# Attention by query halves, and all eight PSUM banks in one pool, in a pre-norm transformer layer

## What is computed

```python
x = x + attn(layernorm(x))     # x: (2, 1024, 1024) fp32
x = x + ffn(layernorm(x))

def attn(x):                   # 32 heads, hd = 32, scale = 32 ** -0.5
    q, k, v = split(x @ qkvw + qkvb)
    probs = softmax(q @ k.T * scale)        # per head, 1024 x 1024
    return (probs @ v) @ ow + ob

def ffn(x):
    return (silu(x @ W_gate.T) * (x @ W_up.T)) @ W_down.T
```

## Time and profile before

| what | us |
|---|---|
| median of 3 runs (2999.91 to 3004.09) | 3000.97 |
| the profiled execution, its own time | 3001.82 |
| span of its profile | 3000.0 |
| TensorE busy in the span | 2954.2 (98%) |
| VectorE busy | 2180.4 (73%) |
| ScalarE busy | 1660.0 (55%) |
| GpSimd busy | 1393.7 (46%) |

### The profile page before, as it was taken

One profiled execution on the slowest core, in us unless ns is written; L12 is line 12 of the kernel. 1 busy time (PEld: TensorE's weight loads), 2 busy tenths in 40 slices (PEclk: granted clock), 3 DMA queues, 4 the chain that ended last, 5 costly groups with the idle time before them and its releaser, 6 DMA issues.

```text
span 3000.0 us, 39212 instructions
## 1 busy us (share of the span) xinstructions
PE 2954.2 (98%) x13728; PEld 2335.6 (78%) x13728; DVE 2180.4 (73%) x3175; ACT 1660.0 (55%) x3039; POOL 1393.7 (46%) x998
## 2 busy tenths in 40 slices
PE   7999999999999999999999999999999999999999
PEld 7777777777777777777677878888888888888887
DVE  6788888888788888888885488866665666555653
ACT  2588877778788888888874143333333323332221
POOL 1346555554555555556552244444354444535730
PEclk9999999999999999999999999999999999999999
DMA  5545445454454554645845735522532223857874
GB/s 205 173 135 163 142 139 184 131 170 128 128 174 131 156 169 140 192 130 150 253 134 178 240 109 193 189 102 100 233 135 100 100 104 118 262 177 252 268 244 132
DMA packets 328376, 492.10 MB, mean 164 GB/s; under 512 B 34746, under 2 KB 178234, under 8 KB 320116
## 3 DMA queue, kind: packets, MB, share of 16 engines
q1 hardware_dynamic: 328180, 489.60, 51.4%
HBM read 318.58 MB, written 169.87 MB: 163 GB/s over the span
## 4 chain that ended last, share of the span: by engine, by line
PE 89%; DVE 6%; DMA 1%; ACT 1%; issue 1%; POOL 1%; SPq 0%; DVEq 0%; ACTq 0%
PE ps L901 20%; PE ps L902 20%; PE ps L903 20%; PE ps L985 7%; PE ps L997 7%; PE ps L1002 7%; PE ps L969 7%; DVE mx L1342 1%; DVE pl L1364 1%; PE ps L935 1%; DVE wl L1316 1%; ACT ph L1124 0%; ACT pu L1123 0%; SPq L1634 0%; DVE bl L1427 0%
## 5 line engine op out<-in xcount | busy, mean ns | idle before, releaser
L1551 POOL TENSOR_TENSOR pl<-pu,ph 128x512 fp32r<-128x512 f32 x504 | 679.6, 1350 | 677.8 <-ACT ph L1124 677.5
L1342 DVE TENSOR_REDUCE mx<-ps 128x1 f32<-128x512 f32 x1024 | 695.6, 685 | 165.9 <-PE ps L969 159.0
L1123 ACT ACTIVATE pu<-ps 128x512 f32<-128x512 f32 x1024 | 617.6, 603 | 281.8 <-PE ps L985 279.0
L1124 ACT ACTIVATE ph<-ps 128x512 fp32r<-128x512 f32 x1024 | 616.8, 602 | 0.0
L1364 DVE TENSOR_TENSOR pl<-pu,ph 128x512 fp32r<-128x512 f32 x520 | 423.9, 817 | 72.3 <-ACT ph L1124 70.9
L901 PE MATMUL ps<-bh,gh 128*128 128x512 f32 x1208 | 471.3, 390 | 5.3 <-DVE bl L1427 2.5
L903 PE MATMUL ps<-bl,gh 128*128 128x512 f32 x1208 | 470.1, 389 | 0.0
L902 PE MATMUL ps<-bh,gl 128*128 128x512 f32 x1208 | 470.0, 389 | 0.0
L985 PE MATMUL ps<-qst,kst 128*128 128x512 f32 x1024 | 404.5, 395 | 4.3 <-ACT ph L1124 3.5
L997 PE MATMUL ps<-ph,vt 128*65 128x512 f32 x1024 | 407.8, 398 | 0.7 <-ACT uu L1130 0.6
L969 PE MATMUL ps<-kst,qst 128*128 128x512 f32 x1024 | 403.4, 394 | 1.6 <-DVE mx L1342 1.3
(11 more groups left out here) (143 smaller groups left out, 5167.7 us busy)
## 6 DMA issues: line engine op xcount, KB each, us to landing
graw<-in_wgu SPq DMA_DIRECT2D x42, 1024.0 KB, 5.2
sraw<-a_d SPq DMA_DIRECT2D x56, 704.0 KB, 4.9
qst<-q_d SPq DMA_DIRECT2D x192, 128.0 KB
kst<-k_d SPq DMA_DIRECT2D x192, 128.0 KB
a_d<-hs SPq DMA_DIRECT2D x88, 256.0 KB, 2.1
traw<-in_wd SPq DMA_DIRECT2D x77, 256.0 KB, 5.3
tt<-in_wd SPq DMA_DIRECT2D x77, 256.0 KB, 5.3
q_d<-stg SPq DMA_DIRECT2D x64, 256.0 KB, 2.5
```

What stands on the lines that cost most here:

```text
L1123: e.activation(pu[sl][:, :], bk[:, :], ACT.Exp, scale=SCALE).then_inc(s["a_p"], 1)
L1124: e.activation(ph[sl][:, :], bk[:, :], ACT.Exp, scale=SCALE).then_inc(s["a_ph"], 1)
L1342: e.reduce_max(mx[:, j % 2, t, half:half + 1], ps[bank_of["a", j, t, half]][:, :], AX.X).then_inc(s["v_mx"], 1)
L1551: e.tensor_tensor(pl[sl][:, :], pu[sl][:, :], ph[sl][:, :], ALU.subtract).then_inc(s["g_pl"], 1)
```

## The change

In the attention's loop the unit's tile is now (half, key tile) with the key tile changing fastest, for `p` and so for `pl` and `ctx`: a head's eight key tiles are done for the first 512 queries, then for the other 512. A new function, `of_prob`, numbers the tiles in that order, and all waits on these tiles use it. The first scores `a` keep their order. Step `u` for the first half now stands in the middle of a head and no longer at its end.

All eight banks are one pool. `p` takes its bank from it by the planner's rule, and so does the context, which has only one open group at a time and takes a bank among 0 to 5 when a half begins. Ahead of the first `a` and behind the last one, the projections keep to banks 6 and 7, as before, and `p` keeps to 0 to 5. The transposes of the second norm wait for the banks' last users through `freed`.

```diff
-        j, t, half = u // 16, u // 2 % TT, u % 2
+        j, half, t = u // 16, u // TT % 2, u % TT
...
-        if t == 0:
+        if u % 16 == 0:
             until("mst", j)
...
+def of_prob(j, t, half):
+    return (j * 2 + half) * TT + t + 1
...
-                    pe.wait_ge("a_ph", n - 2)
-                    e.matmul(ps[(n - 1) % 2][:, :], kst[j % 3][:, tile_of(t)], qst[j % 3][:, halves(half)],
+                    bk_p = claim(bank_of[step], "a_ph", n)
+                    e.matmul(bk_p[:, :], kst[j % 3][:, tile_of(t)], qst[j % 3][:, halves(half)],
                              start=True, stop=True).then_inc(s["p_st"], 1)
...
-                    bk_c, sl = ps[4 + half], (n - 1) % NPU
+                    sl = (n - 1) % NPU
                     vv = vt[j // GH % 2][:, t, j % GH, 0:65]
                     if t == 0:
-                        pe.wait_ge("a_u", 2 * (j - 1) + half + 1)
+                        bk_c = claim(bank_of["ctx", j, half], "a_u", of_part(j, half))
...
-        bank_of, held, left = {}, {}, {n: -1 for n in (2, 3, 6, 7)}
+        bank_of, held, left = {}, {}, {n: -1 for n in range(8)}
...
+            elif what == "ctx" and at_[1] == 0:
+                bank = min((n for n in range(6) if n not in held.values()), key=lambda n: left[n])
+                bank_of["ctx", at_[0], at_[2]] = held["u", at_[0], at_[2]] = bank
             elif step in held:
                 left[held.pop(step)] = i
-            elif what in ("a", "mrow"):
-                bank = min((n for n in left if n not in held.values()), key=lambda n: left[n])
+            elif what in ("a", "mrow", "p"):
+                bank = min((n for n in left if n not in held.values() and (shared or n < 6)), key=lambda n: left[n])
                 bank_of[step], left[bank] = bank, i
```

More of the change, by code:

```diff
@@ L979, in pe_program @@
                     j, t, half = at_
-                    n = of_tile(j, t, half)
-                    if t == 0:
+                    n = of_prob(j, t, half)
+                    if t == 0 and half == 0:
                         pe.wait_ge(f"d_m{j % 2}", 32 * (j // 2 + 1))
                         pe.wait_ge("v_one", 2)
-                    pe.wait_ge("a_ph", n - 2)
-                    e.matmul(ps[(n - 1) % 2][:, :], kst[j % 3][:, tile_of(t)], qst[j % 3][:, halves(half)],
+                    bk_p = claim(bank_of[step], "a_ph", n)
+                    e.matmul(bk_p[:, :], kst[j % 3][:, tile_of(t)], qst[j % 3][:, halves(half)],
                              start=True, stop=True).then_inc(s["p_st"], 1)
@@ L1118, in act_program @@
                     j, t, half = at_
-                    n = of_tile(j, t, half)
-                    bk, sl = ps[(n - 1) % 2], (n - 1) % NPU
+                    n = of_prob(j, t, half)
+                    bk, sl = ps[bank_of["p", j, t, half]], (n - 1) % NPU
                     act.wait_ge("p_st", n)
@@ L1127, in act_program @@
                     j, half = at_
-                    act.wait_ge("p_pv", of_tile(j, TT - 1, half))
+                    act.wait_ge("p_pv", of_prob(j, TT - 1, half))
                     act.wait_ge(f"d_u{j % 2}", 48 * (j // 2))
-                    e.activation(uu[j % 2][:, halves(half)], ps[4 + half][0:65, :], ACT.Copy).then_inc(s["a_u"], 1)
+                    e.activation(uu[j % 2][:, halves(half)], ps[bank_of["ctx", j, half]][0:65, :], ACT.Copy).then_inc(s["a_u"], 1)
                 elif what == "ch":
@@ L1761, in sp_program @@
                     if i:
[L1762 removed]
+                        sp.wait_ge("p_pv", of_prob(ALL - 1, TT - 1, 1))
                     else:
```

19 lines of the change are left out of this document (8 added, 11 removed).

## The result

The changed kernel is slightly slower: 3004.64 us in the median of 20 runs (3000.15 to 3011.78) against 3000.83 for the kernel before in 20 runs beside it (2996.62 to 3005.74). The ratio is 1.0013, with a 95% interval of 1.0007 to 1.0018: 3.8 us more, between 2.1 and 5.4. The forecast was 1.7 us less. The time lies in the range that was given, but the sign was wrong.

The account below looks back on a forecast made before the run. TensorE was taken to bound the whole kernel, so only its waits could change. 14.5 us lifted - 7.1 back - 5.7 new = 1.7 us less: 3000.97 to 2999 us, range 2991 to 3006.

Parts of the forecast that it names:

- Part 1: TensorE's bank waits in the attention: 16.8 us at second scores, fillers, first scores and context openings, of which 14.5 are lifted.
- Part 2: Lifted waits that return where TensorE next waits for the late engine: 7.1 us back, bounds 3 and 11.
- At 520.31: Second scores waiting for ScalarE, 0.91 us idle: once lifted, the joined maxima's wait 1.5 us later grows, 1.2 us back.
- At 389.99: A filler's 0.81 us wait for a maximum: once lifted, 1.1 us come back at the joined maxima of 401.08.
- From 100 to 125 us: VectorE is the limit there; of some 3.7 us lifted, 3.0 us come back at the next maxima.
- Part 3: New waits where contexts open in banks taken from others: 5.7 us, bounds 2.6 us and 12.5 with 2.7.
- The tight kind: Ten openings on the bank of the previous unit's second scores, no filler in between: 0.26 us each, 2.6 us.
- What costs nothing: Waits per matmul, step places and the moved copy cost nothing; the stalls at 1554.55 (2.74 us) and 1627.92 (3.31 us) stay.
- A: Rival: lifted waits stay lifted, lateness being worked off before the next wait; 9 us less, 2992 us; chance 0.19.
- B: Rival: context openings become the bound, half of 48 stalling; 6.1 us slower, 3007 us; chance 0.12.
- C: Rival: TensorE's clock falls behind stalls; four more dips would be 6.4 us, 3006 us; chance 0.03.
- the signs: Expected waits: second scores' `ph` under 1 us, `mx` under 2.5, joined maxima some 11, openings ten to twenty, late stalls unchanged.

Follow-up runs that it names:

- the reserved bank: Changed kernel, but a context's bank is taken three units ahead of its opening and kept free: 3000.09 us against 3000.46 for the kernel before, ratio 0.9995.
- the half order alone: Tiles by query halves as in the changed kernel, but banks given out as in the kernel before: 3000.49 us against 3000.46 before, ratio 1.0005.
- the old start: Changed kernel, but banks as in the kernel before up to the second head's transpose of the maxima (125 us): 3003.13 us against 3000.46 before, ratio 1.0010.

## Why the prediction was wrong

**Part 1, the waits that go: right in size.** Forecast 14.5 us lifted. Side by side, 13.3 us of stalls at second scores, fillers, first scores and context matmuls are gone (5.9 + 3.6 + 3.0 + 0.8), 12.3 without the transfer's wait of 1.0, which was none of a bank's. The rule "more banks, so the wait for the second scores goes" came true to the letter: line 987 has no wait for `ph` left in the matmuls' view.

**Part 2, what comes back: the step that failed.** It says that if the late engine "stays late until TensorE's next wait for it, TensorE waits there instead". Then it asked this of one kind of next wait only, the joined maxima. There it was about right: 7.2 us in the waits' view became 10.1, where the text said "some 11". But the pool makes new next waits. A first score now claims a bank that the exponential frees, a second score one that the maximum frees, and these were never looked up, since I had carried the planner's rule only to the matmuls that stalled before. They came to 5.6 us (3.3 + 2.3). Of these 2.1 stand at 524.76, 666.42, 682.81 and 736.24, one matmul behind the wait that was lifted, and 2.3 at the four second scores that wait for a maximum, the largest at 116.78; the rest is in matmuls behind, small waits and 0.3 us of slow clock. Together with the transposes, 4.1 new less 1.3 gone, 8.4 us of the 12.3 came back, two thirds and not the half that was forecast. The run with the reserved bank says the same or more: of 12.3 us its pool keeps 3.0 against the kernel before or 0.5 against the half order alone, so 9 to 12 came back (that kernel has one bank less to share, which may hold some of it).

At 520.31, where the text gave back 1.2 us at the joined maxima, 0.81 us came back at the first scores and the rest there. The sum for the place was right and its way was not. At 389.99 the text gave back 1.1 us at the joined maxima of 401.08; these wait no longer than before (0.73 us idle for 0.68), and what came back, 0.5 us, stands at the second scores of 394.99. From 100 to 125 us it took 3.0 us back at the maxima, and the transposes have 3.2 there; but 1.2 more stand at the second scores of 116.78 and behind them, so that more came back than had been lifted, as the run with the old start shows by its 1.3 us. Between 655 and 740 the same fault had a price: I had half of the stalls coming back from the maxima, and what brought most back was the next matmul.

**Part 3, the new waits: right.** Forecast 5.7 us. The reserved bank gives 5.5 by the stretch, about 4 without the clock's share, and 3.7 to 4.6 by the medians; side by side it is 5.2. It said ten to twenty waits, and the weight loads show 20. At 486 us it had 2.7 us; the opening had 1.6, the second scores ahead of it 0.4. The tight kind was priced at 0.26 us each, and so it is in the timeline, 0.43 us from start to start where 0.23 is undisturbed, and 0.06 behind it:

```profile
806.53 0.39 PE L971 MATMUL ps<-kst,qst 128*128 128x512 f32 x1
806.96 0.45 PE L999 MATMUL ps<-ph,vt 128*65 128x512 f32 x1
807.25 0.40 PE L1004 MATMUL ps<-pl,vt 128*65 128x512 f32 x1
```

**What costs nothing: right.** The copy in the middle of a head and the half order show no cost in the run with the half order alone. The stall of the earlier trace rows at 1554.55 is there as before (2.73 us at 1559.54). The one at 1627.92 came out at anything from 1.8 to 4.1 us in the profiles, whatever the kernel.

**Rivals.** A, that the lifted waits stay lifted, is refuted: even with the openings' price and the joined maxima both out of the way, the pool gains 1.4 us by the stretch, which is no more than one fall of the clock, and nothing by the median. (The prediction gives A as 2992 us in one place and 2991 in another; its sum makes it 2992.) B names the openings as the bound; they do cost what part 3 said, and with every opening on its tightest place the kernel is at 3007.0, B's time, but as built it is not at that point. C, the clock, holds in small. The text set it aside because "a stall of 0.9 us had none", and in the second profile of the kernel before that very stall had one. In both profiles of the changed kernel one fall stands within the stretch up to 1500 us, behind a wait that had been made longer by a merge (2.01 us at 125.37, 1.42 at 491.08), where the kernel before had one in two profiles: at 1.6 us each, some 0.8 us. The rule that the text cited from the Trainium skill (TensorE: Matmul & The Clock Gate, "A second HAM failure mode: psum-queue depth-cycling") agrees with this trace in part: the clock did fall behind idles that the cycling made, but not as a swing from group to group. All scores cycle through eight banks now, and it still stands at 1.00 over long stretches (window of the changed kernel, columns as above):

```profile
1200.00:1400.00 200.00, 199.94 (x965) 151.60 (x964) 165.94 (x262) 164.72 (x318) 106.19 (x78) 1.00 0.54 158
```

**The sum as the runs have it**, side by side: 12.3 lifted, 8.4 back, 5.2 at the openings: 1.3 us more, where the forecast had 14.5 - 7.1 - 5.7 = 1.7 less. The stretches differ by 2.5 and the medians by 3.8, with an interval from 2.1 to 5.4. What lies between is in part starts less than 0.1 us late and the falls of the clock; the rest may be chance or lie outside the stretch, and that stays open. All the signs that the text named came: no wait of second scores for `ph`, 0.6 us for `mx` at first scores and fillers, 10.1 at the joined maxima, some twenty waits of openings, the two late stalls. Still the sign of the change was wrong, since each spoke of a row that was there before or was foreseen, and the 3.7 us of the two new rows, `ph` at the first scores and `mx` at the second, stood in none of them.

## What to carry to other kernels

When a wait is lifted, find the late engine and look for the next instruction that will wait for it in the changed program, whoever issues it; one shared pool makes every claim such a place, and a gain that moves one matmul on is no gain. With a rotating pool the distance between a buffer's last reader and its next writer is what counts: a group that opens rarely and right behind busy users is best given a buffer that was set aside a few units ahead. And look first at the largest wait, not at the one that the change is about: the joined maxima had 7.2 of 16 us, and moving one step two units later was worth 11 us, once the transfer queue that it passes had been looked at.

## What the hardware showed besides

TensorE's clock fell behind single waits of 1 to 3 us, in some executions and not in others. Of the changed kernel's two profiles it fell in one behind 2.01 us and in the other behind 1.42; in the kernel before it fell behind 0.91 and 0.80 us close together in one of two. Behind the joined maxima's 2.7 us near 1555 it fell in eight profiles of nine. Each fall cost about eight matmuls at 0.43 us from start to start in place of 0.23, 1.6 us. And the small transfers that carry the maxima were held up for 9.5 us by those ahead in SyncE's queue (6.29 us for a pair and 3.24), which TensorE paid with an idle of 10.1 us.
